# A three-phase transformer block on one core: means and attention evicted in another order in phase one, three expert biases added on VectorE in phase three

## What is computed

```
s = qq[:, :, None, :] * kk[:, None, :, :]
attn = jax.nn.softmax(s / s, axis=2)
out = jnp.einsum('bijh,bjhd->bihd', attn, V).reshape(Bn, Sn, Dn)
return out @ wo + bo
```

```
e0 = jax.nn.silu(x @ sw_w1) * (x @ sw_w3) @ sw_w2
e1 = jax.nn.gelu(sym @ me_c1w + me_c1b, approximate=False) @ me_c2w + me_c2b
e2 = h2 @ ce_gen_w + ce_gen_b
e3 = jax.nn.gelu(x @ ml_w1 + ml_b1, approximate=False) @ ml_w2 + ml_b2
stack = jnp.stack([e0, e1, e2, e3], axis=2)
gathered = jnp.take_along_axis(stack, sel[..., None], axis=2)
return (rw[..., None] * gathered).sum(axis=2)
```

## Time and profile before

| what | us |
|---|---|
| median of 3 runs (lowest, highest) | 1606.96 (1606.38, 1611.56) |
| profiled execution, its own time | 1606.52 |
| its span in the trace | 1604.7 |
| PE busy | 1528.0 (95%) |
| DVE busy | 1113.3 (69%) |
| ACT busy | 846.6 (53%) |
| phase A | 0 to about 350 |
| phase C, steady | from about 970 |

### The profile page before, as it was taken

The page is one execution under the profiler, slowest core; times in us unless marked ns, Lnnn a source line. Parts: engine busy times, 40 slices in busy tenths (PEclk is TensorE's granted clock), DMA queues, the critical chain, the costliest instruction groups (busy, mean ns, idle before and its releaser), DMA issues.

```text
span 1604.7 us, 28918 instructions
## 1 busy us (share of the span) xinstructions
PE 1528.0 (95%) x11368; PEld 1088.5 (68%) x11368; DVE 1113.3 (69%) x2228; ACT 846.6 (53%) x1121; POOL 368.2 (23%) x402
## 2 busy tenths in 40 slices
PE   6999999887799999999999899999999999999998
PEld 3333333334466666666657798898989898898987
DVE  5445555556789999999965777666675767666665
ACT  4888888863588888888873242222222222222221
POOL 0000000121455665666461320000000000000000
PEclk8999999996899999999998999999999999999999
DMA  7655555546457576665742100000000000000000
GB/s 146 133 96 107 106 106 98 111 80 105 61 90 110 78 112 95 101 97 79 98 155 67 51 9 14 1 1 14 1 14 1 14 1 14 1 2 13 1 14 14
DMA packets 61439, 96.73 MB, mean 60 GB/s; under 512 B 12707, under 2 KB 29871, under 8 KB 61305
## 3 DMA queue, kind: packets, MB, share of 16 engines
q1 hardware_dynamic: 61304, 94.89, 32.6%
HBM read 25.64 MB, written 4.19 MB: 19 GB/s over the span
## 4 chain that ended last, share of the span: by engine, by line
PE 87%; DVE 6%; ACT 2%; issue 2%; SPq 2%; DMA 1%; POOL 0%; POOLq 0%; DVEq 0%; ACTq 0%
PE ps L109 82%; PE ps L1127 2%; SPq L119 2%; ACT PX L1281 1%; DVE EE L657 1%; ACT H L536 1%; PE ps L1089 1%; PE ps L1135 1%; DVE XC L1945 1%; DVE NM L1336 1%; PE ps L1744 0%; PE ps L1735 0%; DVE XH L571 0%; PE ps L1059 0%; DVE X L583 0%
## 5 line engine op out<-in xcount | busy, mean ns | idle before, releaser
L1336 DVE TENSOR_REDUCE NM<-ps 128x4 f32<-128x1024 f32 x256 | 307.9, 1220 | 46.1 <-PE ps L109 44.7
L1281 ACT ACTIVATE PX<-ps 128x1024 f32<-128x1024 f32 x256 | 262.2, 1024 | 81.0 <-PE ps L109 79.8
L536 ACT ACTIVATE H<-ps,b1c 128x1024 f32<-128x1024 f32 x256 | 268.0, 1117 | 49.5 <-PE ps L109 48.0
L1905 ACT ACTIVATE GF<-ps,cols 128x512 f32<-128x512 f32 x128 | 88.2, 689 | 301.0 <-PE ps L109 300.8
L109 PE MATMUL ps<-XC,W_sw_w 128*128 128x512 f32 x768 | 187.3, 395 | 0.0
L2091 DVE CAST GH<-GF 128x512 fp32r<-128x512 f32 x192 | 82.1, 427 | 146.3 <-ACT GF L1905 143.1
L109 PEld LDWEIGHTS ps<-XC,W_sw_w 128*128 128x128 f32 x768 | 141.5, 190 | 28.3
L2207 POOL TENSOR_SCALAR RSc<-AGc 128x4 f32<-128x4 f32 x23 | 6.9, 298 | 610.4 <-DVE AGc L1994 610.4
L109 PE MATMUL ps<-PX,VT 128*32 128x256 f32 x2048 | 139.6, 391 | 2.2 <-DVE X L583 2.1
L1900 ACT ACTIVATE GF<-ps 128x512 f32<-128x512 f32 x64 | 38.1, 596 | 195.5 <-PE ps L109 195.5
L109 PE MATMUL ps<-KT,QT 48*128 48x512 f32 x512 | 132.1, 515 | 6.8 <-DMA QT<-XSb 3.8
(11 more groups left out here) (238 smaller groups left out, 2569.3 us busy)
## 6 DMA issues: line engine op xcount, KB each, us to landing
ST<-QS SPq DMA_DIRECT2D x256, 96.0 KB, 2.8
KT<-KS SPq DMA_DIRECT2D x128, 192.0 KB, 4.7
QT<-XSb SPq DMA_DIRECT2D x128, 96.0 KB, 4.2
XT<-in_xT_dram SPq DMA_DIRECT2D x8, 512.0 KB, 3.9
raw_a<-in_x_dram SPq DMA_DIRECT2D x8, 512.0 KB, 4.2
CR<-in_ctxT_dram SPq DMA_DIRECT2D x8, 512.0 KB, 5.7
out_dram<-X SPq DMA_DIRECT2D x7, 512.0 KB, 3.0
R_sw_w<-in_sw_w_dram SPq DMA_DIRECT2D x6, 512.0 KB, 4.9
```

The lines of the kernel that those rows point to most:

```text
L536: e.activation(H1[s % 8][:, :, :], PP[s % 3][:, :, :], ACT.Tanh, bias=b1c[:, half:half + 1], scale=1.0).then_inc(act_th, 1)
L1281: e.activation(PX[s % 3][:, :, :, :], PP[2][:, :, :].rearrange("p g (c q) -> p g c q", c=2), ACT.Exp, bias=0.0, scale=0.25).then_inc(act_e ...
L1336: e.tensor_reduce(NM[u % 2][:, qc, :, :, i], PP[qc][:, :, :].rearrange("p g (m k) -> p g m k", m=2), AX.X, ALU.max, negate=True).then_inc( ...
L1905: e.activation(g[:, :], o, f, bias=cols[:, col:col + 1], scale=1.0).then_inc(act_g, 1)
```

## The change

In phase A `means2` moves from J = 12 + 16m to J = 10 + 16m, behind `norms`. It now writes strips of 32 rows (MM is widened, its upper half zero), and DVE evicts all of them by one addition of a tile BO, which holds bo in the rows 16 of the strips and zero elsewhere; this stands behind the KM/SM eviction of the period. After `attend` DVE evicts P[6] first and P[7] second.

In phase C the bias matmuls go. BR now holds the three biases on all 128 partitions, and DVE adds weight times bias to X1 with four instructions for each expert: for pairs 1 to 7 in chunks 11 (me), 12 (gen) and 13 (ml), for pair 0 all twelve in chunk 17. In this dictionary 1, 2, 3 are me, gen and ml. To prepare this at the end of phase B, the two loads v2 and br grow (v2 from 2 KB to 128 KB, br from 6 KB to 384 KB), three memsets on POOL and one tiny load go, and one copy takes the place of three DVE instructions.

```diff
-    MM = put("MM", [128, 2, 4, 16])
+    MM = put("MM", [128, 2, 4, 32])
+    BO = put("BO", [128, 256])
...
     def means2_due(J):
-        return due(J, 12, 16, NP // 2)
+        return due(J, 10, 16, NP // 2)
...
-                    t = mm(e, P[6][32 * b:32 * b + 16, 0:256], MM[:, k, b, :], wvo[:, 1, k, :], k == 0, k == 1)
+                    t = mm(e, P[6][32 * b:32 * b + 32, 0:256], MM[:, k, b, :], wvo[:, 1, k, :], k == 0, k == 1)
...
-            free[6] = (dve_x1, 2 * p + 2)
-            free[7] = (dve_x1, 2 * p + 1)
+            free[6] = (dve_x1, 2 * p + 1)
+            free[7] = (dve_x1, 2 * p + 2)
...
-            for u in (1, 0):
+            for u in range(2):
                 x1 = X1[:, 4 * p + 2 * u:4 * p + 2 * u + 2, :]
...
-        e.memset(MB[:, :], 0.0).then_inc(dve_init, 1)
+        e.memset(MM[:, :, :, :], 0.0).then_inc(dve_init, 1)
+        e.memset(BO[:, :], 0.0).then_inc(dve_init, 1)
...
-                for b in range(4):
-                    e.tensor_copy(MB[32 * b:32 * b + 16, :], P[6][32 * b:32 * b + 16, 0:256]).then_inc(dve_mb, 1)
+                e.tensor_tensor(MB[:, :], P[6][:, 0:256], BO[:, :], ALU.add).then_inc(dve_mb, 1)
...
+ADDS = 28
+FIRST_BIASES = {17: (1, 2, 3)}
+BIASES = {11: (1,), 12: (2,), 13: (3,)}
...
-        def bias(o, row):
-            w.wait_ge(dve_br, 1)
-            w.wait_ge(pool_init, 3)
-            return mm(e, o, ONE[:, :], BR[:, row, :], False, True)
...
-                bias(o, 1).then_inc(pe_gen, 1)
...
-                for v in tiles:
-                    t = bias(P[4 + v // 2][:, 256 * (v % 2):256 * (v % 2) + 256], row)
...
+        def add_bias(j, k):
+            w.wait_ge(dve_br, 1)
+            w.wait_ge(dve_add, ADDS * j + 4 * k)
+            for v in range(4):
+                e.scalar_tensor_tensor(out=X1[:, 4 * j + v, :], in0=BR[:, k - 1, :], scalar=PB[:, v, k:k + 1], in1=X1[:, 4 * j + v, :],
+                                       op0=ALU.mult, op1=ALU.add).then_inc(dve_add, 1)
...
+            for k in (BIASES if j else FIRST_BIASES).get(i, ()):
+                add_bias(j, k)
             if i == 14:
                 ff_add(j)
             if i == 18:
-                add_expert(j, 1, 24 * j + 15, 16 * j + 4)
+                add_expert(j, 1, 24 * j + 15, ADDS * j + 16)
```

More of the change, by code:

```diff
@@ L690, in vector @@
                     e.tensor_scalar(SM[:, :, 1, :], o.rearrange("q (g t) -> q g t", g=4), KM[:, 1:2], None, ALU.mult).then_inc(dve_sm, 1)
+            m = means2_due(J)
+            if m is not None:
+                w.wait_ge(pe_mb, m + 1)
+                w.wait_ge(pe_att, 2 * m)
+                w.wait_ge(d_bo, 64)
+                e.tensor_tensor(MB[:, :], P[6][:, 0:256], BO[:, :], ALU.add).then_inc(dve_mb, 1)
             pr = project_due(J)
@@ L1408, in step @@
                 elif f == 9:
-                    t = e.tensor_tensor(br[:, 1, :], br[:, 1, :], o[0:2, 0:256], ALU.add)
+                    t = e.tensor_tensor(br[:, 1, :], br[:, 1, :], o[:, 0:256], ALU.add)
                 else:
@@ L1669, in early @@
                     w.wait_ge(*end)
[L1670 to L1671 removed]
+                for o, i in ((BC[:, 1:3, :], a["BC"][:, 1:3, :]), (bf, a["BC"][:, 3, :]), (RB[:, :, :], a["RB"]), (gc[:, :, :], a["gc"])):
                     dma(e, o, i, d_tc)
@@ L1809, in second @@
             x, hc = chunk(i)
-            name, row, last = {"sw": ("sw_w2", None, 7), "ce": ("ce_f2w", None, 3), "me": ("me_c2w", 0, 3), "ml": ("ml_w2", 2, 7)}[x]
+            name, last = {"sw": ("sw_w2", 7), "ce": ("ce_f2w", 3), "me": ("me_c2w", 3), "ml": ("ml_w2", 7)}[x]
             g = GH[n % 4]
@@ L1822, in second @@
                     else:
-                        w.wait_ge(dve_add, 16 * j + 2 * u + {"sw": -2, "ce": 2, "ml": 6}[x])
+                        w.wait_ge(dve_add, ADDS * j + 2 * u + {"sw": -2, "ce": 2, "ml": 18}[x])
                 t = mm3(e, o, g[:, 0, 128 * v:128 * v + 128], g[:, 1, 128 * v:128 * v + 128], wt[:, 0, hc % 4, :], wt[:, 1, hc % 4, :],
-                        hc == 0 and v % 2 == 0, hc == last and row is None)
-            if hc == last and row is not None:
-                for v in tiles:
-                    t = bias(P[4 + v // 2][:, 256 * (v % 2):256 * (v % 2) + 256], row)
-                t.then_inc(done, 1)
-            elif done is pe_second:
+                        hc == 0 and v % 2 == 0, hc == last)
+            if done is pe_second or hc == last:
                 t.then_inc(done, 1)
@@ L1968, in rows @@
             w.wait_ge(b_end["folds"], 10)
[L1969 to L1974, removed]
+            for end in gathered:
+                w.wait_ge(*end)
+            e.tensor_copy(BR[:, :, :], br[:, :, :]).then_inc(dve_br, 1)
         def synergy(j):
@@ L2183, in gpsimd @@
         one = Serial(w)
-        def init():
-            for end in gathered:
-                w.wait_ge(*end)
-            one.wait()
-            one.done(e.memset(f32(BR[:, :, :]), 0.0), pool_init)
-            one.wait()
-            one.done(e.memset(f32(ONE[:, :]), 0.0), pool_init)
-            one.wait()
-            one.done(e.memset(f32(ONE[0:2, :]), 1.0), pool_init)
         def take(name, q):
```

62 lines of the change are left out of this document (26 added, 36 removed).

## The result

| what | before | changed |
|---|---|---|
| median (lowest to highest) of 4 runs | 1606.95 (1606.38 to 1611.56) | 1594.77 (1592.93 to 1598.66) |
| ratio, 95% interval | | 0.990 [0.9855, 0.9944] |
| profiled execution, span | 1606.5, 1604.7 | 1598.66, 1596.9 |
| PE busy / DVE busy | 1528.0 / 1113.3 | 1523.8 / 1141.8 |

The median fell by 12.2 us; 13.7 were forecast (1592.8).

What follows compares the result with a forecast made beforehand. The prediction took PE to bound the kernel, without gaps in phase C and with waits in phase A. Its terms summed to -13.7 us, from 1606.5 to 1592.8 us; range 1588.5 to 1599.5 for 8 in 10.

Steps and rivals of the forecast that it cites:

- means2, m = 0 to 2: Phase A: J = 28 loses 2.29 us, J = 26 grows by 0.71; net 1.58 for each m, minus 4.7 us.
- means2, m = 3: Phase A, J = 58 to 60: means2 takes the place of prep_x's wait, ACT limits the rest; zero, between -1 and +1.
- attend, eight times: Phase A: with P[6] evicted first, w2 starts 0.60 us earlier after each of eight attends; minus 4.8 us.
- start: Kernel start: one more DVE memset ahead of the projections whose eviction PE waits for; plus 0.3 us.
- phase C from pair 1 on: Phase C: bias matmuls go at 0.118 us each; DVE's additions hidden, except plus 1.3 us waiting for expert me.
- phase C, pair 0: Twelve additions in chunk 17 make PE wait: plus 3.8 us, and plus 1.7 for a clock fall; bias matmuls saved.
- seam between B and C: End of phase B: larger loads and the new copy hidden by score steps; zero, up to +1 us.
- rival (a): Phase C, pair 0: the clock doesn't fall in the gap; 1.7 us less, 1591.1 us; chance 0.24.
- rival (b): Phase C, chunks 11 to 13: additions don't fit, PE waits at chunk 15; plus 4, 1596.8 us; chance 0.12.
- Rival (d): Phase C: three SBUF operands make additions much dearer, so slower than before; 1615 us at 0.65 us each; chance 0.03.
- (c): Phase A's gains don't reach phase B; 3 to 9.2 us lost, up to 1602; chance 0.14, shared with (e).
- (e): Phase A: w2 waits for something other than the bank, so neither move gains; 1602 us; chance 0.14, shared with (c).

Runs made afterwards that it cites:

- e6: Changed kernel with means2 back at J = 12 + 16m, its eviction still one addition: 1594.27 us, ratio 0.9899 to the kernel before.
- r2: The changed kernel run again without any edit, beside the kernel before on one chip: 1593.73 us, ratio 0.9909.
- e8: Changed kernel with pair 0's biases in chunks 19, 21, 23, means2 of m = 3 in J = 60, expert me's addition before chunk 18's split: 1586.38 us, ratio 0.9857.
- e5: Changed kernel with the old eviction order after attend, P[7] first and P[6] second: 1601.90 us, ratio 0.9959 to the kernel before.
- e10: Kernel before with one edit, P[6] evicted first after attend and P[7] second: 1606.22 us, ratio 0.9971.
- e4: Changed kernel with pairs 1 to 7 also adding all twelve biases in chunk 17: 1636.13 us, ratio 1.0154 to the kernel before.
- e1: Kernel before with the phase A edits alone, phases B and C as before: 1600.95 us, ratio 0.9926.
- e9: Changed kernel with the three biases left out altogether, neither additions nor bias matmuls: 1591.32 us, ratio 0.9882 to the kernel before.
- e7: Changed kernel with bias additions placed differently from pair to pair, one or two groups late or two groups in chunk 12: one run, 1602.68 us.

## Why the prediction was right

| term | forecast | measured |
|---|---|---|
| means2, m = 0 to 2 | -4.7 | 3 x (3.99 + 7.05 - 4.58 - 4.77) = -5.1 |
| means2, m = 3 | 0 (-1 to +1) | +0.7 in the two profiles of the changed kernel, about 0 over all 14 (below) |
| attend, eight times | -4.8 | 8 x (1.34 - 0.75) = -4.7 |
| start | +0.3 | +0.3 (QS wait 3.71 instead of 3.41) |
| phase C from pair 1 on | 88 x -0.118 + 1.3 = -9.1 | 6 x -1.12, and -1.56 from pair 7's start to the end = -8.3 |
| phase C, pair 0 | 8 x -0.118 + 3.8 + 1.7 = +4.6 | 103.09 - 98.76 = +4.3 |
| seam between B and C | 0 (up to +1) | no cost seen: J = 62 to the first `W_ce,XC` takes 529.8 before, 530.0 twice in the changed kernel |
| sum | -13.7 | -12.8; timed -12.2 and -14.6 |

(Of the 96 bias matmuls 8 stood ahead of pair 1's first matmul: me and gen of pair 0. The row for pair 0 is the stretch from its first `W_ce,XC` to pair 1's. The two profiled executions are only 7.9 us apart, not 12.8: the late DMA and its fall, some 3.5 us, stand in no row, and 1.4 us of scatter is assigned to nothing. So the table is an account of the terms, and the timed medians decide on the whole.)

**Means2.** J = 28 came out as forecast (4.77 for 4.76). J = 26 was forecast at 4.70 and took 4.58: `means2` starts 0.39 us behind `norms` where I let it start behind all of `norms`' 0.53. The margin ahead of `w2` is the one forecast, under 0.1 us. What I gave as one edit is two, and e6 shows that the cheap eviction carries three quarters.

**J = 58.** The forecast said that `means2` takes the place of a wait there, and that ACT holds the rest. From `norms` of J = 58 to the second `prep_x` behind it it took 20.93 and 20.95 us (r2) where before took 20.23: +0.7. But over all 14 profiles this stretch takes 19.50 to 20.95 us with `means2` in J = 58 (eight profiles, mean 20.5) and 18.44 to 21.78 with `means2` in J = 60 (six, mean 20.4). What moves it most is the clock behind the gap of some 2.15 us: it falls in 13 of the 14 (`w2` 2.69 to 3.64 us), and 18.44 is e8, the one without a fall. So the zero stands, and the +0.7 is no price of the move that could be told from this scatter. That ACT holds the rest was not tested.

**Attend.** The new eviction order gains its 0.59 us all eight times (the last one: `PX,VT` waits 1.50 us for X instead of 2.09). What the prediction left out is the clock: 7 falls behind 24 gaps of 0.72 us against none behind the new order without a late DMA. That speaks for a gain above 4.8 us; e5 shows 8.2, e10 4.7, and how much it is on average stays open.

**Pair 0.** The gap was forecast at 3.8 and is 3.77, with the queue as described: twelve additions, GH of chunk 18, then expert me. The fall was the forecast's choice against rival (a); all 14 gaps of 3.75 to 3.83 us in the profiles (pair 0 in six profiles, and all eight pairs of e4) have a fall behind them., from which I argued, was a poorer guide than I took it for (last section): one gap spoke for a fall and a longer one against it, so that this term came out right in part by luck.

**Pairs 1 to 7.** The step of four additions is 1.67 us as taken, and rival (b) didn't occur. The waits for expert me are 0.27 us a pair, forecast 0.17 (of which seven make 1.2 us, where the sum has 1.3): that is the mis-sized term, 0.7 us of the 0.8 that are missing here. Rival (d) is answered by the group of DVE's additions out of SBUF, 479 ns each against 476 for those out of PSUM:

```profile
L2050 DVE SCALAR_TENSOR_TENSOR X<-BR,PB,X 128x256 f32<-128x256 f32 x96 | 40.0, 479 | 0.1
```

**Rivals (c) and (e)** seemed borne out by the first profile, in which phase A and B delivered 3.9 us of 9.2. The timing of e1 refutes (c): 11.9 us less with phase A alone, at least 7.7. The rows refute (e): `w2` starts as soon as the bank is free after `attend`, and has no wait behind `means2`. What the first profile lacked was one execution's late DMA, and r2 starts phase C 8.4 us earlier than before; by itself that would say little, given the scatter of phase B.

## What to carry to other kernels

Where one bank of two is wanted next, evict it first: here it cost nothing, since the other bank's next user stood far behind, and gave nearly the whole time of the other eviction (0.59 us of 0.65). Work may be moved to an engine with idle time up to that idle time, chunk by chunk: 1.67 us of additions in 1.67 us of idle time cost nothing (e9), 1.67 more cost 1.3 (e7), and all of it in one chunk ahead of what TensorE waits for costs 5 to 6 (e4); so look at what stands behind it in the queue. And don't read a difference of a few microseconds from one profile against another: compare distances within a profile, and repeat the profile before explaining a wait that appears once.

## What the runs showed of the hardware

The same idle gap of TensorE sometimes costs a fall of the clock and sometimes doesn't: 0.72 us, 7 of 24; 2.12 us, 1 of 2 in one execution; 2.1 to 2.3 us at J = 58, 13 of 14; 3.8 us, 14 of 14. A fall costs 1.2 to 1.7 us behind the gaps of 0.72 us and in pair 0, some 2.2 behind the late DMA, and 1.5 and 2.6 in turns in e4. The kernel before, unaltered, ran `w2` behind the attend of J = 30 in 1.92 us in its first profile and in 3.57 in its second. The Trainium skill ("TensorE: Matmul & The Clock Gate", "Part 1: The HAM clock gate") says of the start of a kernel that the number of matmuls at the low rate differs from run to run of the same kernel. What the traces show here is the same kind of difference, behind gaps in the middle.

More regular are the two gaps of the earlier trace rows, of 3.04 and 1.76 us. In the changed kernel, timeline of PE:

```profile
885.35 0.97 PE L109 MATMUL ps<-wob,OH 128*128 128x256 f32 x6 [3.04 <-DVE OH L1368]
886.15 4.50 PE L109 MATMUL ps<-XC,W_sw_w 128*128 128x512 f32 x12
...
904.69 0.98 PE L109 MATMUL ps<-wob,OH 128*128 128x256 f32 x6 [1.76 <-DVE OH L1368]
905.50 2.94 PE L109 MATMUL ps<-XC,W_sw_w 128*128 128x512 f32 x12
```

Before, the clock fell behind the second and not the first; here it is the other way round. In all 14 profiles it fell behind exactly one of the two, eight times the first and six times the second. So the length of a gap alone didn't decide, and the price of this pair of gaps was 1.4 to 1.6 us in every run (twelve matmuls in 4.34 to 4.51 us instead of 2.94). Why one fall excludes the other no run here tells.
